# Attention by autocorrelation: lags in four shares with two levels of sums, row statistics on ScalarE, ctx's constant row on GpSimd

## The reference

```python
def _autocorrelation(Q, K, V):            # Q = layernorm(x), K = V = ctx, 8 heads
    qf, kf = fft(q, axis=2), fft(k, axis=2)
    corr = ifft(qf * conj(kf), axis=2).real        # 512 lags for every channel
    w, idx = top_k(corr.transpose(0, 1, 3, 2), 12)  # int(2 * log(512)) lags
    w = softmax(w)
    for i in range(12):
        g = minimum(idx[..., i] + pos, L - 1)
        out += w[..., i] * take_along_axis(v, g, axis=2)
x = x + _autocorrelation(layernorm(x), ctx, ctx)
x = x + ffn(layernorm(x))                 # 64 experts of rank 8, top 16 gates
```

## Time and profile before

| | |
|---|---|
| median of 3 runs | 2340.18 us (2336.01 to 2342.96) |
| the profiled execution's own time | 2341.09 us |
| span of its profile | 2339.3 us |
| TensorE (PE) busy | 2265.3 us, 97% of the span |
| VectorE (DVE) busy | 1874.8 us, 80% |
| ScalarE (ACT) busy | 1031.9 us, 44% |
| GpSimd (POOL) busy | 1567.8 us, 67% |
| granted clock of TensorE, mean | 0.991 |

### The profile page before, as it was taken

How to read it: one execution, slowest core, us unless ns; L and a number is a source line. 1 busy time by engine, 2 the same in 40 slices (tenths; PEclk the granted TensorE clock), 3 DMA queues, 4 the chain that set the end, 5 groups by cost and what they waited for, 6 DMA issues and landing times.

```text
span 2339.3 us, 29526 instructions
## 1 busy us (share of the span) xinstructions
PE 2265.3 (97%) x9664; PEld 1549.1 (66%) x9664; DVE 1874.8 (80%) x3947; ACT 1031.9 (44%) x1872; POOL 1567.8 (67%) x997
## 2 busy tenths in 40 slices
PE   4999999999999999999999998799999999999999
PEld 2566566566556656656656655577778777887787
DVE  6999999999999999999998998765656566666652
ACT  3453453453454454454454444444444443444441
POOL 4998998998998898898998986523343333333330
PEclk9999999999999999999999998899999999999999
DMA  6232232232233233233222125534444444444431
GB/s 227 95 117 95 93 119 95 84 125 98 77 113 117 77 113 117 77 113 114 80 87 89 59 80 201 197 126 163 159 160 166 161 152 161 170 155 152 160 126 54
DMA packets 110413, 288.04 MB, mean 123 GB/s; under 512 B 7136, under 2 KB 7264, under 8 KB 109152
## 3 DMA queue, kind: packets, MB, share of 16 engines
q1 hardware_dynamic: 110304, 286.72, 35.7%
HBM read 219.58 MB, written 67.11 MB: 123 GB/s over the span
## 4 chain that ended last, share of the span: by engine, by line
PE 88%; DVE 9%; DMA 1%; issue 1%; ACT 1%; POOL 1%; SPq 0%; DVEq 0%; ACTq 0%
PE pair L625 14%; PE lag L597 7%; PE out L499 6%; PE out L501 5%; PE out L500 5%; PE evac L541 5%; PE z L499 5%; PE z L501 5%; PE evac L566 5%; PE pair L554 5%; PE evac L565 5%; PE z L500 5%; PE pair L499 4%; PE pair L500 4%; PE pair L501 4%; PE tp L511 2%
## 5 line engine op out<-in xcount | busy, mean ns | idle before, releaser
L1307 POOL TENSOR_TENSOR r_f<-prod 128x1024 f32<-128x1024 f32 x128 | 303.8, 2384 | 120.6 <-DVE prod L845 77.7
L1341 POOL TENSOR_TENSOR rows<-rows,cin 128x1024 f32<-128x1024 f32 x48 | 115.7, 2411 | 363.9 <-DMA rows<-out_dram 294.3
L625 PE MATMUL pair<-r_f,back 128*128 128x512 f32 x768 | 335.4, 592 | 0.0
L625 PEld LDWEIGHTS pair<-r_f,back 128*128 128x128 f32 x768 | 145.7, 190 | 169.4 <-issue 167.8
L597 PE MATMUL lag<-lags,p_f 128*128 128x256 f32 x1024 | 233.1, 381 | 3.4 <-DVE e L866 2.6
L499 PE MATMUL pair<-w_hi,wts_hi 128*128 128x512 f32 x512 | 210.0, 410 | 9.8 <-DVE prod L845 7.2
L597 PEld LDWEIGHTS lag<-lags,p_f 128*128 128x128 f32 x1024 | 192.8, 191 | 30.6 <-issue 4.6
L499 PE MATMUL out<-b_hi,zt_hi 128*128 128x512 f32 x512 | 209.6, 409 | 1.6 <-ACT zt_hi L1250 1.5
L499 PE MATMUL z<-a_hi,xt 128*128 128x512 f32 x512 | 206.5, 403 | 0.4 <-DVE a_lo L795 0.4
L500 PE MATMUL pair<-w_lo,wts_hi 128*128 128x512 f32 x512 | 200.9, 392 | 0.0
L501 PE MATMUL out<-b_hi,zt_lo 128*128 128x512 f32 x512 | 200.8, 392 | 0.0
(11 more groups left out here) (157 smaller groups left out, 5422.9 us busy)
## 6 DMA issues: line engine op xcount, KB each, us to landing
vf<-in_ctx_dram SPq DMA_DIRECT2D x32, 1024.0 KB, 5.1
out_dram<-att_sb SPq DMA_DIRECT2D x32, 1024.0 KB, 4.2
rows<-out_dram SPq DMA_DIRECT2D x64, 512.0 KB, 3.6
cin<-out_dram SPq DMA_DIRECT2D x64, 512.0 KB, 4.1
xin<-in_x_dram SPq DMA_DIRECT2D x64, 512.0 KB, 3.9
out_dram<-rows SPq DMA_DIRECT2D x64, 512.0 KB, 2.6
xf<-in_x_dram SPq DMA_DIRECT2D x30, 1024.0 KB, 5.1
stat_in<-in_x_dram SPq DMA_DIRECT2D x28, 1024.0 KB, 5.1
```

The costliest lines, as they stand in the source:

```text
L625: return nc.tensor.matmul(pair_ps[:, bank, :], back[:, 3 * bank + n, :], r_f[:, row, :], start=n == 0, stop=n == 2)
L1307: nc.gpsimd.tensor_tensor(dst, prod[:, slot, 0:2, :], prod[:, slot, 2:4, :], ALU.add).then_inc(add_done, 1)
```

## The change

The 512 lags are stored as four runs of 128: column blocks hold what is computed as even-even, even-odd, odd-odd and odd-even shares. Each share needs one row of `p_f` and 128 columns of `lags`, so that a tile is four products of 128, 128, 129 and 127 columns, each alone in its columns, instead of four of 256 that add up in pairs. Two levels of sums follow: the first joins the cosine shares and the sine shares (lag n and 256-n), the second gives n and 256+n as before. ScalarE copies the cosine half first, and after the first level the low half. The weights' tables and `fold_w` follow the new order. The row statistics of all but the first batch become sums and sums of squares about a near mean on ScalarE, with `later_means` on VectorE in the steps with r = 3. The constant row is scaled on ScalarE and added on GpSimd.

```diff
-                for part, cols in enumerate((slice(0, L // 2), slice(L // 2, L))):
-                    for par in range(2):
-                        last = nc.tensor.matmul(lag_ps[t % 2][:, cols], p_f[:, 2 * par + part, ch], lags[:, par, cols],
-                                                start=par == 0, stop=par == 1)
+                for cols, row in ((slice(0, P), 0), (slice(P, 2 * P), 2), (slice(2 * P, 3 * P + 1), 3),
+                                  (slice(3 * P + 1, L), 1)):
+                    last = nc.tensor.matmul(lag_ps[t % 2][:, cols], p_f[:, row, ch], lags[:, cols], start=True, stop=True)
...
 SyncE
-                if is_step(i, 0):
-                    sp.wait_ge(stat_used, LT * 2)
-                    load_stat(k, r, stat_in[:], stat_loaded)
-                if (i - 2) // GPB + 2 < B:
-                    sp.wait_ge(stat_used, LT * (i + 3))
-                    load_stat((i - 2) // GPB, (i - 2) % GPB, stat_in[:], stat_loaded)
+                for g in (1, 2) if is_step(i, 0) else (3, 4) if is_step(i, 1) else (i + 3,):
+                    if g < GPB * (B - 1):
+                        sp.wait_ge(stat_used, LT * (g + 1))
+                        load_stat(g // GPB - 1, g % GPB, stat_in[:], stat_loaded)
...
 VectorE
+            def later_means(m):
+                mean, var = norm_x[0][:, :, 0], norm_x[0][:, :, 1]
+                sums, squares, off, off_square = (total_x[:, n, :] for n in range(4))
...
+                nc.vector.tensor_reduce(sums, sum_x[:], mybir.AxisListType.X, ALU.add).then_inc(mean_step, 1)
+                nc.vector.tensor_reduce(squares, square_x[:], mybir.AxisListType.X, ALU.add).then_inc(mean_step, 1)
+                dve.wait_ge(mean_step, done + 2)
+                nc.vector.scalar_tensor_tensor(off, sums, 1.0 / D, near_mean[:], ALU.mult, ALU.add).then_inc(mean_step, 1)
+                dve.wait_ge(norm_ready, NORM_OPS * m)
+                nc.vector.tensor_scalar(mean, sums, 1.0 / D, None, ALU.mult).then_inc(norm_step, 1)
+                dve.wait_ge(mean_step, done + 3)
+                nc.vector.tensor_tensor(off_square, off, off, ALU.mult).then_inc(mean_step, 1)
+                dve.wait_ge(mean_step, done + 4)
+                nc.vector.scalar_tensor_tensor(var, squares, 1.0 / D, off_square, ALU.mult, ALU.subtract).then_inc(norm_step, LT - 1)
...
                 def sums_of(tiles):
                     for second in (0, 1):
                         for t in tiles:
-                            even, odd = lag_ps[t % 2][:, 0:L // 2], e[:, t, L // 2:L]
...
+                            if not second:
+                                dve.wait_ge(cos_copied, CT * i + t + 1)
+                                op = nc.vector.tensor_tensor(cos_ps, cos_in, sin_ps, ALU.add)
+                            else:
+                                dve.wait_ge(lag_folded, corr_at(i, t, 0))
+                                op = nc.vector.tensor_tensor(sin_ps, cos_in, sin_ps, ALU.subtract)
+                            op.then_inc(lag_folded, 1)
+                    for second in (0, 1):
+                        for t in tiles:
...
+                            if not second:
+                                dve.wait_ge(low_copied, CT * i + t + 1)
+                                op = nc.vector.tensor_tensor(total, high, low, ALU.add)
+                            else:
                                 dve.wait_ge(corr_summed, corr_at(i, t, 0))
+                                op = nc.vector.tensor_tensor(low, high, low, ALU.subtract)
                             op.then_inc(corr_summed, 1)
...
-                    if s:
-                        first_statistics()
                     evac_sin(1)
-                    nc.vector.scalar_tensor_tensor(v_cyc[cur][0:1, 0, :], v_last[0:1, :], float(L), v_cyc[cur][0:1, 0, :],
-                                                   ALU.mult, ALU.add).then_inc(dc_ready, 1)
...
-                if s and not is_step(i, 0):
-                    statistics(stat_in, r, i, (2, 3))
-                    if r == 3:
-                        hold(stat_used, LT * (i + 3))
-                        means(k + 2)
+                if s and r == 3:
+                    later_means(k + 2)
...
 ScalarE
+            def row_sums(g):
+                act.wait_ge(stat_loaded, 16 * (g + 1))
+                if g % GPB == 0 and g > 0:
+                    act.wait_ge(norm_step, NORM_STEPS * (g // GPB) + LT)
+                for j in range(LT):
+                    nc.scalar.activation(stat_in[:, j, :], stat_in[:, j, :], ACT.Copy,
+                                         accum_out=sum_x[:, j, g % GPB:g % GPB + 1]).then_inc(stat_summed, 1)
+                if g % GPB == 0:
+                    act.wait_ge(stat_summed, LT * (g + 1))
+                    nc.scalar.activation(near_mean[:], sum_x[:, :, 0], ACT.Copy, scale=-1.0 / CH).then_inc(near_done, 1)
+            def row_squares(g):
+                act.wait_ge(stat_summed, LT * (g + 1))
+                act.wait_ge(near_done, g // GPB + 1)
+                for j in range(LT):
+                    nc.scalar.activation(stat_in[:, j, :], stat_in[:, j, :], ACT.Square, bias=near_mean[:, j:j + 1],
+                                         accum_out=square_x[:, j, g % GPB:g % GPB + 1]).then_inc(stat_used, 1)
...
+                def lag_copies(tiles):
                     for t in tiles:
                         act.wait_ge(lag_ready, CT * i + t + 1)
-                        nc.scalar.activation(e[:, t, L // 2:L], lag_ps[t % 2][:, L // 2:L], ACT.Copy).then_inc(odd_copied, 1)
+                        nc.scalar.activation(e[:, t, 0:2 * P], lag_ps[t % 2][:, 0:2 * P], ACT.Copy).then_inc(cos_copied, 1)
+                    for t in tiles:
+                        act.wait_ge(lag_folded, corr_at(i, t, 1))
+                        nc.scalar.activation(e[:, t, 2 * P:L].rearrange("p (h n) -> p h n", n=P),
+                                             lag_ps[t % 2][:].rearrange("p (h s n) -> p h s n", s=2, n=P)[:, :, 1, :],
+                                             ACT.Copy).then_inc(low_copied, 1)
...
                     evac_from(0, evac_neg(i, 0), v_neg[cur][:, 0, :])
+                    nc.scalar.activation(dc_last[:], v_last[0:1, :], ACT.Copy, scale=float(L)).then_inc(dc_scaled, 1)
...
                     norm(k, r, 2, range(LT))
+                if is_step(i, 0):
+                    row_sums(0)
+                    row_squares(0)
+                elif is_step(i, 1):
+                    row_sums(2)
+                    row_squares(2)
+                if i > 0 and i + 2 < GPB * (B - 1):
+                    row_sums(i + 2)
+                    row_squares(i + 2)
...
                     for t in (0, 1):
                         weigh(i, t)
+                if is_step(i, 0):
+                    row_sums(1)
+                    row_squares(1)
...
 GpSimd
+                if t % 2 == 1:
+                    both = slice(t - 1, t + 1)
+                    nc.gpsimd.tensor_copy(pick[:, both, 0:L:2 * P], e[:, both, 2 * P::-2 * P]).then_inc(w_folded, 1)
+                    up, down = e[:, both, P:P + 1], e[:, both, 3 * P:3 * P + 1]
+                    nc.gpsimd.tensor_tensor(pick[:, both, P:P + 1], up, down, ALU.add).then_inc(w_folded, 1)
+                    nc.gpsimd.tensor_tensor(pick[:, both, 3 * P:3 * P + 1], up, down, ALU.subtract).then_inc(w_folded, 1)
...
                         add_products(prod_x(i, n), n, p_f[:, 2 * n:2 * n + 2, :])
+                    pool.wait_ge(dc_scaled, i + 1)
+                    dc = v_cyc[(r + 1) % 2][0:1, 0, :]
+                    nc.gpsimd.tensor_tensor(dc, dc, dc_last[:], ALU.add).then_inc(dc_ready, 1)
```

More of the change, by code:

```diff
@@ L68, in transform_tables @@
     ones = -np.stack([sin(2 * pi * np.outer(t, neg[par]) / (2 * L)).sum(0) for par in range(2)], 1)
[L70 removed]
+    evens, odds = [], []
     for par in range(2):
[L72 to L75 removed]
+        even = 2.0 * cos(2 * pi * np.outer(cyc[par], np.arange(P + 1)) / L) / L
+        odd = -2.0 * sin(2 * pi * np.outer(cyc[par], np.arange(P + 1)) / L) / L
         odd[:, 0] = 0.0
         if par == 0:
+            even[0] = alt(np.arange(P + 1)) / L
             odd[0] = 0.0
[L79 removed]
+            even -= even[:, P:]
+        evens.append(even)
+        odds.append(odd)
+    lags = [evens[0][:, :P], evens[1][:, :P], odds[1], odds[0][:, 1:P]]
+    near = [p, np.where(p == 0, P, H - p)]
     wts = []
@@ L87, in transform_tables @@
                     f[0] = H
-                m = fn(2 * pi * np.outer(p + P * half, f) / L)
+                m = fn(2 * pi * np.outer(near[half], f) / L)
                 if fn is cos:
@@ L100, in transform_tables @@
             for half in range(2):
-                m = fn(2 * pi * np.outer(p + P * half, neg[par]) / (2 * L))
+                m = fn(2 * pi * np.outer(near[half], neg[par]) / (2 * L))
                 if half == 0 and fn is sin:
@@ L303, in build_program @@
         W_BLOCKS = (2, 3, 0, 1)
+        W_FOLDS = 14
         SPLITS = 2
```

(15 more changed lines are left out.)

54 lines of the change are left out of this document (26 added, 28 removed).

## The result

The changed kernel takes **2369.51 us** (median of 4 runs, 2368.40 to 2372.34) against 2340.81 for the kernel before (4 runs): a ratio of 1.0127, 95% interval 1.0109 to 1.0146. It is slower, by 28.7 us; 2383 was forecast, and the range held it. The profiled execution took 2370.08 us, its span is 2368.3, 29.0 more than before.

What follows compares the result with a forecast made beforehand. It took TensorE to bound the kernel, VectorE's loop nearly as long. From 2341.1: +9 +4 (start), +43 +2 (closing steps), -13 -2 (ordinary, last steps) gave 2384, less 0.9 to the median 2383; range 2360 to 2412.

Steps and rivals of the forecast that it cites:

- rival 1: Weight loads bound TensorE's 128-column lag records at 0.19 us, steps take 44.7 us, the kernel 2423 us; chance 0.10.
- Ordinary steps: Attention steps that finish no batch's statistics: forecast to go from 44.1 to 43.4 us, bound by VectorE.
- rival 2: VectorE's second-half sums are not in its loop; GpSimd sets steps of 41.3 us, the kernel takes 2320 us; chance 0.14.
- Closing steps: Attention steps finishing a batch's statistics (i = 2, 6, ..., 26): forecast 51.9 us against 44.75 in six, +2 in step 26.
- rival 4: Square on ScalarE needs another function table: 1.3 us more per closing step and at the start, 2393 us; chance 0.05.
- Rival 3: Statistics hurt only by half: later_means 0.9 us, ScalarE 1 to 2 us sooner in closing steps, 2348 us; chance 0.09.
- 1.33 becomes 3.3: VectorE's lag sums for the second half (two tiles) of a step, in its loop, grow from 1.33 to 3.3 us.
- it stands 5.1 us: In a closing step VectorE finishes its six stages at T+26 and waits 5.1 us for ScalarE, until T+31.
- T: The start of the weight transposes on TensorE in a step, from which times within the step are counted.
- 7.6 - 2.7 - 1.2 + 1.3 + 0.6 = 5.6: VectorE's stretch before the weight products: 7.6 us, less constant row and two statistics, plus lag sums and copy wait.
- the one full wait that was counted: In closing steps, later_means on VectorE waits once for a whole GpSimd operation, 3.4 us in all (0.9 to 7.6).
- The forecast's start (+9, +4): ScalarE's extra statistics, two groups each in step 0 and step 1, lengthen these steps by 9 and 4 us.

Runs made afterwards that it cites:

- e1: The kernel before with only the constant row moved, scaled on ScalarE and added on GpSimd: 2330.51 us, ratio 0.9962.
- e6: The changed kernel with the constant row put back on VectorE: 2366.78 us, ratio 1.0069.
- e4: The changed kernel with three of later_means' four operations behind the reductions written tile by tile on one element, the mean left on four: 2376.43 us.
- e9: e7 with the last two tiles of a step back on the 256-column correlation and the constant row back on VectorE: 2329.57 us, ratio 0.9957.
- e8: The changed kernel with the four groups of the second batch's statistics on VectorE as before: 2359.77 us, ratio 1.0027.
- e7: The changed kernel with the row statistics back on VectorE, placed where its rows have idle time: 2314.46 us, ratio 0.9893.
- e12: e9 with the constant row off VectorE again, scaled in place on ScalarE and added on GpSimd: 2290.18 us, ratio 0.9761.
- e3: The changed kernel with ScalarE taking a closing step's statistics before its normalization of x instead of behind it: 2348.47 us, ratio 0.9988.
- e11: e3 with every later_means operation behind the reductions written tile by tile on one element: 2335.95 us, ratio 0.9979.

## Why the prediction was right

**The mechanism held.** Lag records are 0.111 us apart (0.108 forecast), not 0.19: rival 1 is out. Ordinary steps are led by VectorE, with no gap from the last weight product to the v_neg correction and TensorE waiting ahead of x's second spectrum and v_neg's last product: rival 2 is out. Closing steps wait for ScalarE at the choice, and step 0 reads ctx's spectrum late, at 74.08 (73.7 forecast, 64.53 before). Square brought no table load: in the attention stage the lines view has 8 ahead of exponentials and 7 ahead of roots, before as after, so rival 4 is out. Rival 3 had later_means at 0.9 us and ScalarE's lateness small; they were 3.2 and 3.0 us. Two sizes that were off in the same step mostly cancel, as told below, so the 2383 is nearer than its terms. Its range is narrower than its own terms: added straight they give some 2356 to 2425 where it says 2360 to 2412; the result lies in both.

**Sizes that were off,** which make the 13.5 us between 2383 and 2369.5:

- "1.33 becomes 3.3", the second half's sums: measured 2.87. The hand-over to ScalarE in the middle costs 0.2 (the third pair of sums starts 0.87 behind the second, the others 0.66 to 0.67 apart) where I took 0.6. That is the 0.4 us by which ordinary steps are shorter, 43.04 instead of 43.4, and 6 of the 13.5 us. Another 2.3 are the step of 46.40 in the kernel before, which was no part of the forecast.
- "it stands 5.1 us": measured 3.0, and 4.65 in step 18. ScalarE came as forecast (T+30.6 against T+31), but VectorE's six stages ended at T+27.6 instead of T+26: TensorE's 24 remaining weight products took 7.2 us (688.48 to 695.68) instead of the 5.6 of an ordinary step (736.25 to 741.82), for its lower clock. I had them at full speed in a step in which I had just made TensorE wait. As ScalarE sets the moment, what VectorE is late only shortens its stand. Of the 0.9 us by which the step is shorter than forecast (51.0 against 51.9; 5.4 in six), 0.4 are ScalarE's and 0.4 the second half's sums.
- "7.6 - 2.7 - 1.2 + 1.3 + 0.6 = 5.6": the term of 2.7 for the constant row was no property of the row. Moved alone it brings 0.3 us a step (e1), and put back into the changed kernel it costs nothing (e6). Of the 41.0 us that I called VectorE's work, 2.1 were this wait. The sum came out right at T+6.7 (T+6.5 forecast), as ScalarE's copies stand there in its place, and TensorE's first weight spectrum is complete only at T+6.45 (733.21 + 0.39). The sum held because a row that has moved away can't wait either; what was wrong was to count it as a gain of the change, since e6 has the same steps with the row in place.
- later_means: 3.2 us (3.4 forecast), by the one full wait that was counted, and on the last but one of its operations, the square; in e4 it fell on the mean and in e6 on the first of them with two inputs (1.74), so it could as well have been another.

The durations of VectorE's operations that met GpSimd's folds: with two SBUF inputs 2.34 us on four elements and 2.86 on 512, with one input on four elements 2.05, on one element 0.14 to 0.21. The Trainium skill (SBUF — State Buffer, section Who interferes with whom) lets VectorE contend with GpSimd where it reads two SBUF inputs, or one in a two-port mode, and says that issue order decides who blocks. The trace agrees on the first two, and on the third in the kernel before and in e6, down to GpSimd's 2.82 there; in e9 a row drawn 0.06 us ahead of the fold waited all the same. I had read the first of these as a fixed price.

The forecast's start (+9, +4) measured +9.5 and +3.0. With the second batch's statistics back on VectorE (e8), 7.3 of the 9.5 and 2.7 of the 3.0 us are gone; the other 2.3 of step 0 come with the correlation, for which the forecast had nothing there, and ScalarE's delay covers them.

Left open: why one of two constant rows, each drawn 0.06 to 0.07 us ahead of the same fold, waits and the other does not; the profile does not show the order in which they were granted. Open too is why the clock fell in some closing steps and not in others behind the same stand.

## What to carry to other kernels

When one engine is relieved, read the room of the next one first: here 3.4 us a step off TensorE were worth nothing until VectorE's work moved into its own idle time (e7), and the last 24 us (2314.46 to 2290.18) came from giving TensorE back half of what had been taken off it (e12). Work moved to an idle engine must be placed by what that engine's queue holds behind it: the same statistics ahead of a wait instead of behind it gave 21 us (2369.51 to 2348.47, e3). And a stretch at a low clock costs only where nobody comes later still: it was free in the changed kernel and cost 1.6 us a step in e3. A long duration of a small operation on VectorE was here a wait, not work: look at what GpSimd began just before, and don't book it as a saving.

## What the runs showed of the hardware

- Whether a VectorE operation waits for a whole GpSimd one, or two, turns on a tenth of a microsecond of phase, and the steps repeat their phase: of the 29 rows from 120 to 1400 us all wait before (2.86 us in the mean), none in e6 (0.71), part of them in e9 (2.02). The 12 runs of e9 lie within 18 us; the 5 of e12, which differs by the row alone, within 0.5.
- A plain float32 product of 128 columns with a load of its own takes 0.111 us a record (two records a product), nearly as fast as the transposes (0.109).
- A lower granted clock (0.72 or 0.86 over the 12 us from T+10, with products 0.43 instead of 0.23 us apart) followed TensorE's stand of 3.1 to 3.2 us ahead of the weight products in six of the seven closing steps of the changed kernel and in five of seven in e3, and a stand of 2.0 us in two of seven in e11. In the kernel before, where TensorE stands 0.7 us there, and in e7 (1.1), the clock stayed at 1.00 in all seven. A fall costs 1.6 us where VectorE waits for these products, and nothing where ScalarE comes later still.
